# First expert layer of an eight-layer kernel: the routing of a group of tokens is chosen two groups ahead of the token list, with the shared expert's products in another order between, and the ones over the places in 24 comparisons of one choice each

## The reference

```python
def _gate(xf, gate_w):
    logits = xf @ gate_w.T
    scores = jax.nn.softmax(logits.astype(jnp.float32), axis=-1)
    top_w, top_i = lax.top_k(scores, TOP_K)
    return ((top_w * ROUTE_SCALE).astype(xf.dtype), top_i)
...
order = jnp.argsort(e_flat)
counts = jnp.zeros((E,), jnp.int32).at[e_s].add(1)
starts = jnp.concatenate([jnp.zeros((1,), jnp.int32), jnp.cumsum(counts)[:-1]])
pos = jnp.arange(T * TOP_K, dtype=jnp.int32) - starts[e_s]
valid = pos < CAP
buf_idx = jnp.where(valid, e_s * CAP + pos, E * CAP)
xbuf = jnp.zeros((E * CAP + 1, D), xf.dtype).at[buf_idx].set(xf[t_s])
h = jax.nn.silu(jnp.einsum('ecd,edi->eci', xb, w1)) * jnp.einsum('ecd,edi->eci', xb, w3)
...
shared = jax.nn.silu(xf @ sw1) * (xf @ sw3) @ sw2
```

## Time and profile before

| | |
|---|---|
| median of 3 runs | 2593.61 us (2591.57 to 2594.86) |
| profiled execution | 2603.1 us, of it a span of 2601.3 us |
| PE, DVE, ACT, POOL busy, share of the span | 78%, 69%, 54%, 47% |
| mean granted clock of TensorE over the span | 0.876 |
| first shared product to the first routed expert | 336.39 to 456.76 us |

### The profile page before, as it was taken

One profiled execution on the slowest core, in us unless ns is written; L12 is line 12 of the kernel. 1 busy time (PEld: TensorE's weight loads), 2 busy tenths in 40 slices (PEclk: granted clock), 3 DMA queues, 4 the chain that ended last, 5 costly groups with the idle time before them and its releaser, 6 DMA issues. The chain is left out here.

```text
span 2601.3 us, 42510 instructions
## 1 busy us (share of the span) xinstructions
PE 2031.6 (78%) x13337; PEld 1244.3 (48%) x13434; DVE 1800.6 (69%) x4006; ACT 1406.1 (54%) x3553; POOL 1214.8 (47%) x1425
## 2 busy tenths in 40 slices
PE   6999667999699999999999738906855535888487
PEld 3444344665366777777677535603422222333144
DVE  4898455575689999899998643327837665888454
ACT  1777311452487888888888603303644431677443
POOL 4443000443788888888887554265512122333100
PEclk9999578999899999999999959956876665899799
DMA  4565300784302500001000032238830005576100
GB/s 138 160 184 155 110 8 11 244 259 150 64 17 91 206 19 21 18 19 23 16 16 3 4 157 83 74 126 228 228 104 1 1 36 149 137 194 180 54 1 33
DMA packets 264487, 242.05 MB, mean 93 GB/s; under 512 B 37002, under 2 KB 236141, under 8 KB 263629
## 3 DMA queue, kind: packets, MB, share of 16 engines
q1 hardware_dynamic: 237996, 187.71, 24.8%
q0 software_dynamic: 13776, 36.59, 5.1%
q10 hardware_dynamic: 12496, 15.03, 1.7%
HBM read 141.95 MB, written 98.19 MB: 92 GB/s over the span
## 5 line engine op out<-in xcount | busy, mean ns | idle before, releaser
L736 DVE TENSOR_REDUCE a_nm<-bank 128x2 f32<-128x512 f32 x640 | 409.1, 683 | 39.5 <-PE bank L602 37.2
L844 ACT ACTIVATE a_PT<-bank 128x512 f32<-128x512 f32 x640 | 355.1, 602 | 141.4 <-PE bank L609 125.4
L602 PE MATMUL bank<-a_stack_k,a_stack_q 48*128 48x256 bf16 (+2 forms) x1280 | 262.5, 298 | 98.2 <-DVE a_nm L736 60.6
L2836 PE MATMUL bank<-f_w,f_zc 128*128 128x512 bf16 x1074 | 267.3, 384 | 28.0 <-DVE f_zc L2944 18.8
L3156 POOL TENSOR_TENSOR f_hr<-f_hr,half_pow 128x4 f32<-128x4 f32 x192 | 244.7, 1275 | 84.2 <-DVE f_hr L2953 84.0
L609 PE MATMUL bank<-a_stack_q,a_stack_k 51*128 51x256 bf16 (+2 forms) x1280 | 252.2, 289 | 8.3 <-ACT a_PT L844 7.7
L3048 ACT ACTIVATE f_Pm<-bank,f_nmax 128x128 f32<-128x128 f32 x512 | 183.0, 384 | 76.0 <-DVE f_nmax L2968 75.1
L602 PEld LDWEIGHTS bank<-a_stack_k,a_stack_q 48*128 48x128 bf16 (+2 forms) x1280 | 92.1, 99 | 259.4 <-DVE a_nm L736 174.8
L624 PE MATMUL bank<-a_PT,a_V 128*32 128x256 f32 x2560 | 187.3, 414 | 1.4 <-ACT a_PT L844 1.4
L1684 POOL DMA_INDIRECT m_xe<-moe_in,m_token x64 | 76.1, 1190 | 217.0 <-DVE m_token L1566 132.5
L2836 PEld LDWEIGHTS bank<-f_w,f_zc 128*128 128x128 bf16 x1152 | 112.4, 99 | 123.8 <-issue 26.5
(11 more groups left out here) (364 smaller groups left out, 4807.5 us busy)
## 6 DMA issues: line engine op xcount, KB each, us to landing
cut<-a_parts SPq DMA_DIRECT2D x96, 192.0 KB
cut<-a_parts SPq DMA_DIRECT2D x144, 128.0 KB
o<-a_O SPq DMA_DIRECT2D x32, 512.0 KB, 3.8
top_in<-zero SPq DMA_DIRECT2D x8, 2048.0 KB, 19.2
a_stack_q<-cut SPq DMA_DIRECT2D x64, 192.0 KB
a_stack_k<-cut SPq DMA_DIRECT2D x64, 192.0 KB
m_w<-in_w SPq DMA_DIRECT2D x32, 368.0 KB
moe_out<-m_oe ACTq DMA_DIRECT2D x32, 256.0 KB
```

The costliest lines, as they stand in the source:

```text
L602: x = t.matmul(ps[:, n * D:(n + 1) * D], self.stack_q[rows, i, slot, n * P:(n + 1) * P], self.stack_k[rows, i, slot, :], start=True, stop= ...
L736: v.tensor_reduce(self.nm[:, g % 2, :, at % self.J, at // self.J], self.k.bank[h % 3][:, :].rearrange("p (n m) -> p n m", n=2), AX.X, ALU. ...
L844: a.activation(self.PT[:, h % 8, :, :].rearrange("p m n -> p (m n)"), self.k.bank[3 + h % 3][:, :], ACT.Exp).then_inc(self.a_exp.sem, 1)
L2836: x = t.matmul(ps[:, :], self.zc[:, b % 2, j, c_, :], self.fp8.w3[:, m, c_, at:at + BANK], start=(m == 0 and c_ == 0), stop=(m == 2 and c_ ...
```

## The change

Three things are changed, and no arithmetic but that of the comparison's form.

1. The order on DVE, PE and ACT. `choose` of group g + 2 is now at the end of group g's round and `places` of group g + 1 before it. Before the loop stand `places` of group 0 and `choose` of group 1. Part 0 of the shared expert for the next group is put ahead of `shared_down` of this one. On PE, `tokens` is now ahead of `counts`, and the first `counts` comes after the transposes of group 2 instead of before them.
2. Banks: the logits of group 1 go to bank 4, the counts from group 1 on to bank 1. Waits are added on PE for the banks that are shared (`v_who` or `a_T` in `tokens`, `v_lg` in part 1 of group 0).
3. `at_place` was one `tensor_tensor` of 3072 elements with float32 inputs. It is now 24 `tensor_scalar` of 128 elements with a bf16 input (`count16`, a copy of the numbers 0 to 127), each against a scalar per partition.

```diff
--- before.py
+++ after.py
@@ -1147,7 +1147,7 @@
             self.topi, self.topf, self.ntop = s("topi", [P, B, 8], U32), s("topf", [P, B, 8]), s("ntop", [P, B, 2])
             self.hot = s("hot", [P, NG, TOP_K, N_EXP])
             self.hit = s("hit", [P, self.GROUPS + 1, 1 + NG, N_EXP], BF16)
-            self.count, self.lane = s("count", [P, P]), s("lane", [P, 1])
+            self.count, self.count16, self.lane = s("count", [P, P]), s("count16", [P, P], BF16), s("lane", [P, 1])
             self.cut, self.cutf = s("cut", [P, 2, NG, TOP_K], U32), s("cutf", [P, 2, NG, TOP_K])
             self.in_tile, self.at_place = s("in_tile", [P, NG, TOP_K, 2, TILES], BF16), s("at_place", [P, NG, TOP_K, P], BF16)
             self.who = s("who", [P, P])
@@ -1240,19 +1240,22 @@
         t.wait_ge(self.d_par.sem, self.d_par.at(6))
         for g in range(self.GROUPS):
             self.transposes(t, g)
+            if g == 2:
+                self.counts(t, 0)
             self.logits(t, g)
-            if g == 1:
-                self.counts(t, 0)
         t.wait_ge(self.d_sw.sem, self.d_sw.at(3))
+        self.shared_up(t, 0, 0)
         for g in range(self.GROUPS):
-            self.shared_up(t, g, 0)
+            more = g + 1 < self.GROUPS
             self.shared_up(t, g, 1)
-            if g + 1 < self.GROUPS:
+            self.tokens(t, g)
+            if more:
                 self.counts(t, g + 1)
-            self.tokens(t, g)
-            if g + 1 == self.GROUPS:
+            self.shared_up(t, g, 2)
+            if more:
+                self.shared_up(t, g + 1, 0)
+            else:
                 self.turn_tokens(t)
-            self.shared_up(t, g, 2)
             self.shared_down(t, g, 0)
             self.shared_down(t, g, 1)
         for e in range(N_EXP + 2):
@@ -1276,7 +1279,7 @@
 
     def at_bank(self, g):
 
-        return self.k.bank[1 if g else 7][:, g * self.NG * N_EXP:(g + 1) * self.NG * N_EXP]
+        return self.k.bank[{0: 7, 1: 4}.get(g, 1)][:, g * self.NG * N_EXP:(g + 1) * self.NG * N_EXP]
 
     def logits(self, t, g):
         ps = self.at_bank(g)
@@ -1301,12 +1304,17 @@
         x.then_inc(self.p_cnt.sem, 1)
 
     def at_bank_of_counts(self, g):
-        return self.k.bank[5 if g == 0 else 0][:, g * self.NG * N_EXP:(g + 1) * self.NG * N_EXP]
+
+        return self.k.bank[1 if g else 5][:, 0:self.NG * N_EXP]
 
     def tokens(self, t, g):
 
         ps = self.k.bank[0]
         t.wait_ge(self.v_hot.sem, self.v_hot.at(g + 1))
+        if g:
+            t.wait_ge(self.v_who.sem, self.v_who.at(g))
+        else:
+            t.wait_ge(self.a_T.sem, self.a_T.at(2 * self.GROUPS))
         for i in range(self.NG * TOP_K):
             b, j = divmod(i, TOP_K)
             x = t.matmul(ps[:, 0:P], self.in_tile[:, b, j, :, :].rearrange("p m n -> p (m n)"), self.at_place[:, b, j, :],
@@ -1323,6 +1331,8 @@
         pa, pb = self.k.bank[2 + 2 * (u % 2)], self.k.bank[3 + 2 * (u % 2)]
         xg = self.xnT[:, :, 4 * g:4 * g + 4, :].rearrange("p c b t -> p c (b t)")
         t.wait_ge(self.a_T.sem, self.a_T.at(2 * g + 2))
+        if u == 1:
+            t.wait_ge(self.v_lg.sem, self.v_lg.at(2))
         if u >= 2:
             t.wait_ge(self.a_sg.sem, self.a_sg.at(u - 1))
         for c_ in range(DC):
@@ -1399,19 +1409,18 @@
         self.normalise(v, 2)
         v.wait_ge(self.d_par.sem, self.d_par.at(6))
         c.mark(v.tensor_copy(self.tri[:, :], self.trif[:, :]))
+        c.mark(v.tensor_copy(self.count16[:, :], self.count[:, :]))
         c.mark(v.memset(self.hit[:, 0, 0, :], 0.0))
         v.tensor_copy(self.ones16[:, :], k.ones[:, :]).then_inc(self.v_one.sem, 1)
         self.weights(v, 0)
         self.choose(v, 0)
         self.slots(v, 0)
+        self.places(v, 0)
+        self.weights(v, 1)
+        self.choose(v, 1)
+        self.shared_product(v, 0, 0)
         for g in range(G):
             more = g + 1 < G
-            if more:
-                self.weights(v, g + 1)
-            self.shared_product(v, g, 0)
-            if more:
-                self.choose(v, g + 1)
-            self.places(v, g)
             self.shared_product(v, g, 1)
             if g:
                 self.shared_add(v, g - 1, 0)
@@ -1419,9 +1428,15 @@
             self.gather_tokens(v, g)
             if more:
                 self.slots(v, g + 1)
+            self.shared_product(v, g, 2)
+            if more:
+                self.places(v, g + 1)
+                self.shared_product(v, g + 1, 0)
             else:
                 self.end_tokens(v)
-            self.shared_product(v, g, 2)
+            if g + 2 < G:
+                self.weights(v, g + 2)
+                self.choose(v, g + 2)
         self.shared_add(v, G - 1, 0)
         self.shared_add(v, G - 1, 1)
         self.fp8.parameters(v)
@@ -1467,7 +1482,7 @@
         sl = slice(NG * g, NG * (g + 1))
         ntop, e = self.ntop, self.ex[:, :, :]
         lg = self.at_bank(g).rearrange("p (b e) -> p b e", b=NG)
-        v.wait_ge(self.p_lg.sem, self.p_lg.at(self.GROUPS if g else 1))
+        v.wait_ge(self.p_lg.sem, self.p_lg.at(self.GROUPS if g >= 2 else g + 1))
         c.mark(v.tensor_reduce(ntop[:, sl, 0], lg, AX.X, ALU.max))
         c.after()
         v.tensor_tensor(e, lg, self.spread(ntop[:, sl, 0], N_EXP), ALU.subtract).then_inc(self.v_lg.sem, 1)
@@ -1529,23 +1544,26 @@
         c, NG = self.k.dve, self.NG
         sl = slice(NG * g, NG * (g + 1))
         slot, tile = self.combine.slot[:, sl, :], self.in_tile
+        v.wait_ge(self.v_slot.sem, self.v_slot.at(g + 1))
         if g:
             v.wait_ge(self.p_who.sem, self.p_who.at(g))
-        else:
-            v.wait_ge(self.v_slot.sem, self.v_slot.at(1))
         c.mark(v.tensor_scalar(self.cut[:, 0, :, :], slot, 7, None, ALU.logical_shift_right))
         c.mark(v.tensor_scalar(self.cut[:, 1, :, :], slot, P - 1, None, ALU.bitwise_and))
         c.after()
         c.mark(v.tensor_copy(self.cutf[:, :, :, :], self.cut[:, :, :, :]))
         c.after()
...
         for i in range(NG):
             c.mark(v.tensor_scalar(tile[:, i, :, 1, :], tile[:, i, :, 0, :], float(NG * g + i), None, ALU.mult))
         c.after()
         c.mark(v.tensor_scalar(tile[:, :, :, 0, :], tile[:, :, :, 0, :], self.lane[:, 0:1], None, ALU.mult))
-        v.tensor_tensor(self.at_place[:, :, :, :], count(P), self.spread(self.cutf[:, 1, :, :], P), ALU.is_equal).then_inc(self.v_hot.sem, 1)
+        for n in range(NG * TOP_K):
+            i, j = divmod(n, TOP_K)
+            x = v.tensor_scalar(self.at_place[:, i, j, :], self.count16[:, :], self.cutf[:, 1, i, j:j + 1], None, ALU.is_equal)
+            if n < NG * TOP_K - 1:
+                c.mark(x)
+        x.then_inc(self.v_hot.sem, 1)
         c.after()
 
     def gather_tokens(self, v, g):
@@ -1606,11 +1624,15 @@
             self.copy_T(a, g)
             if g == 1:
                 self.exp(a, 0)
+        self.exp(a, 1)
+        self.shared_silu(a, 0, 0)
         for g in range(self.GROUPS):
+            self.shared_silu(a, g, 1)
+            self.shared_silu(a, g, 2)
             if g + 1 < self.GROUPS:
-                self.exp(a, g + 1)
-            for n in range(3):
-                self.shared_silu(a, g, n)
+                self.shared_silu(a, g + 1, 0)
+            if g + 2 < self.GROUPS:
+                self.exp(a, g + 2)
         for e in range(N_EXP + 3):
             if e < N_EXP:
                 self.copy_xeT(a, e)
```

More of the change, by code:

```diff
@@ L1540, in places @@
         c.after()
[L1541 to L1542 removed]
+        c.mark(v.tensor_tensor(tile[:, :, :, 0, :], self.count[:, 0:TILES].unsqueeze(1).unsqueeze(1).to_broadcast([P, NG, TOP_K, TILES]), self.spread(self.cutf[:, 0, :, :], TILES), ALU.is_equal))
         c.after()
```

2 lines of the change are left out of this document (removed).

## The result

| | |
|---|---|
| median of the changed kernel's 4 runs | 2559.94 us (2554.08 to 2567.47) |
| before, 4 runs | 2594.24 us (2591.57 to 2596.19) |
| ratio | 0.987, 95% interval 0.9842 to 0.9899 |
| its profiled execution | 2561.87 us, span 2560.1 us |

The kernel is 34 us faster, and clear of noise. The forecast was 46 us, 2547.6 us, with a range from 2538 to 2560. The direction was right, the size a third too large. The ratio set against the median before gives 2560.5 us, just outside the range.

The account below looks back on a forecast made before the run. In the stretch from PE's first shared product to its first routed expert, PE and DVE take turns. The last add comes 47.7 us sooner, less 1.7 us: 2593.6 - 46 = 2547.6 us, range 2538 to 2560.

Parts of the forecast that it names:

- The bound and the chain: Shared expert: PE and DVE take turns; PE waits 2.63, 7.07 and 0.85 us a group, behind DVE's `choose` and `places`.
- The head: Start of the stretch: transposes ahead of `counts` fill PE's wait, so the shared products start 2.4 us earlier.
- DVE sets the round: Each group: DVE's round of 19.0 us is longer than PE's 17.3 and sets the pace, instead of 30.84 us.
- My sum of the other parts: DVE's round besides comparisons: products 1.80, adds 1.20, `gather_tokens` 0.20, `slots` 3.00, `places` 3.64, `weights` 0.60 and 0.40, `choose` 5.89 us.
- The price of the comparisons: In `places` on DVE: 24 small comparisons at 0.095 us each, 2.3 us, replace the wide one of 3.27 us.
- Rival 1: Comparisons in `places` are slow, 0.22 us each; saving falls to about 40 us, 2553.6 us; chance 12 in 100.
- So nothing is exposed there: End of the stretch: the first expert's gathered rows are ready at 408.5 us, just ahead of the last add at 408.9.
- my discount: 1.7 us taken off the saving for added waits, the copy `count16` and small slips between DVE and PE.
- The clock: PE's clock stays at 1.00 from about 339 us to the stretch's end; waits up to 1.7 us would not lower it.

Follow-up runs that it names:

- the repeated run: The changed kernel measured once more with no edit; median 2554.78 us, ratio 0.985 to the kernel before.
- The early turn: Changed kernel with the wide comparison and, in the last group, the token list turned on PE right behind `tokens`; 2553.21 us, ratio 0.9826 to before.

## Why the prediction was right in direction and too large in size

**The bound and the chain** were right. The three waits of PE and what the low clock cost behind them were the stretch's loss. Inside the rounds the order took away those ahead of `tokens` and `shared_down`, and left one of 1.8 to 3.1 us ahead of `counts`. The wide comparison in the new order gives all that the change gives.

**The head** was right: the first shared product came 25.1 us behind the first transposes, against 27.6 before, 2.5 us where I had 2.4.

**DVE sets the round** was right, and shown from both sides: 0.63 us more in the comparisons make the round 0.63 us longer, and half of them on another engine make it 1 us shorter. My sum of the other parts was 16.7 us; the measured round of 20.53 less 3.90 is 16.6.

**The price of the comparisons is the first term that was mis-sized.** In *The comparison* I took 0.095 us for one, "nearer to the lower end, since the bf16 row is the one that shares the element type". It measured 0.163 us, 3.90 us for 24 instead of 2.3. That is 1.6 us in each of two rounds, 3.2 us. The last add came at 103.3 in the stretch in the repeated run, where I had it at 100.1 (408.9 less 308.81): this term is the whole difference. Rival 1, with 0.22 us for one, came half true. The form decides more than the type: the neighbours 0.08 us apart had a constant as scalar, and this one reads it from memory. The float32 row of L2923 shared that with it and was the better neighbour. The Trainium skill's count ("VectorE: DVE Perf Modes", "Side-by-side: where the cycles go for N=2048 bf16"), by which I gave 0.20 us, is nearer for this form than my price, and too high for the form with a constant, which took 0.105 us here. Its consequence, that the edit alone loses, was right: 0.63 us, where its count made it 1.5.

**"So nothing is exposed there" is the step that failed.** I set the list's end and the first expert's two gathers against the last add, and they did fit: the first transposes were released by the add. But PE's program does the transposes of the second expert ahead of the first expert's products, and of the third ahead of the second's. Four and six gathers, 1.3 us apart, had to be there, and before the change they had 10 us for it. From the last add to the first `expert_down` 7.2 us passed before, 11.7 and 12.6 us after, in part a wait for rows and in part the low clock behind it. That is 4.6 to 5.5 us where I had put nothing: 1.87 us of wait in the first trace and 3.86 in the repeated run, and the rest low clock. With the wide comparison and the clock at 1.00 only the wait is left, 2.58 us, and 9.7 us pass. The early turn makes the list 2.3 us sooner, and as its last add is 1.75 us later, the gathers have 4.1 us more. Both the waits and the low clock are gone there, and 7.2 us pass again, which shows the cause.

The two together are 8.7 us in the repeated run, and 47.7 less 8.7 is the 39.0 us that its stretch gained. Of them my discount had 1.7. The rest of the gap to the first runs' 34 us is scatter of what follows the stretch (2130.0 to 2141.5 us).

**The clock** came back as forecast, for the most part. It still fell in single rounds in some executions and not in others, and cost the last add up to 3.3 us. My reason, that a wait shorter than 2.63 us is too little to bring it down, did not hold: it fell behind 1.80 us in one execution and not behind 3.10 us in another.

**The range** was too narrow. It took in one slow comparison, but no wait at the end of the stretch, which I had reasoned away with one condition where there were three.

## What to carry to other kernels

When a loop gets shorter, look at what ran in its shadow, and count every transfer that the next engine's program asks for up to the first long piece of work, not the first one alone. To price a small operation take the neighbour with the same operands, a scalar read from memory with a scalar read from memory, before one with the same element type. And split a change that has two parts: here the order alone gave all of the gain, and the comparisons took a little away.

## What the runs showed that I had not expected

A longer wait of PE did not make the old stretch longer. With 7.71 us of wait instead of 7.07 the round stayed at 30.95 us. In both kernels the low clock began while PE stood still, and with the longer wait 1.4 us less of the work behind it lay at that clock.

A comparison of 128 elements against a scalar per partition took VectorE 0.163 us and GpSimd 0.69 us. GpSimd took 0.94 us for one in the kernel where VectorE ran its own wide comparison beside it, and VectorE's four operations on `in_tile` 0.99 us instead of 0.77. Both figures of GpSimd are means of two rates. Its windows in that kernel (stretch, length, busy time with the number of comparisons, clock, DMA) are of the time in which VectorE is at `in_tile` and its own comparison, and of what follows:

```profile
350.00:355.20 5.20, 4.86 (x3) 1.00 0.00 0
355.30:361.80 6.50, 6.27 (x10) 1.00 0.00 1
```

One of the 12 counts in both. One takes about 1.6 us beside those operations and 0.6 us behind them, while VectorE goes on with `choose`. So what an engine's operation costs next to another's work depends on which operations those are; which of VectorE's slows it was not tested apart.
